# First attention of a two-layer cross-attention kernel: heads paired as neighbours, queries and keys of a pair by one product in a row half instead of two in quarters

## The reference, cut to what matters

```python
def _proj(W, b, x):
    return jnp.einsum('oi,bil->bol', W, x) + b[:, None]
q = _proj(Wq, bq, x_query)              # x_query = layernorm(x), (32, 64, 512)
k = _proj(Wk, bk, x_key)                # x_key = x_value = ctx
v = _proj(Wv, bv, x_value)
qh = q.reshape(B, D, h, Lh).transpose(2, 0, 1, 3)      # h = 8, Lh = 64, D = 64
scores = jnp.einsum('hbdk,hbek->hbde', qh, kh) * scale
p = jax.nn.softmax(scores, axis=-1)
xh = jnp.einsum('hbde,hbek->hbdk', p, vh)
x = xh.transpose(1, 2, 0, 3).reshape(B, D, L)
return _proj(Wo, bo, x)                 # added to x
```

## Time and profile before

| what | before |
|---|---|
| median of 3 runs | 810.43 us |
| the profiled execution | 810.15 us, its span 808.3 us, mean granted TensorE clock 0.941 |
| TensorE products busy | 687.0 us (85% of the span) |
| TensorE loads busy | 357.8 us (44%) |
| VectorE busy | 621.2 us (77%) |
| ScalarE busy | 483.1 us (60%) |
| GpSimd busy | 364.2 us (45%) |

### The profile page before, as it was taken

The page is one execution under the profiler, slowest core; times in us unless marked ns, Lnnn a source line. Parts: engine busy times, 40 slices in busy tenths (PEclk is TensorE's granted clock), DMA queues, the critical chain, the costliest instruction groups (busy, mean ns, idle before and its releaser), DMA issues. The chain is left out here.

```text
span 808.3 us, 17679 instructions
## 1 busy us (share of the span) xinstructions
PE 687.0 (85%) x6606; PEld 357.8 (44%) x6633; DVE 621.2 (77%) x1028; ACT 483.1 (60%) x873; POOL 364.2 (45%) x271
## 2 busy tenths in 40 slices
PE   2799999999977767499999479999999999479944
PEld 1345454554545555244444134444444444145541
DVE  4687788888636667499998579999999999355456
ACT  1687867667525657277777247787878787422100
POOL 1000008999925664022212146767777776343100
PEclk9999999999999999599999969999999999879955
DMA  5043555555442331023343100000000000035305
GB/s 149 27 136 111 200 186 147 157 147 154 89 126 77 72 82 30 15 56 74 74 71 70 37 0 1 2 2 0 2 1 2 2 1 1 1 72 85 53 2 208
DMA packets 94504, 54.98 MB, mean 68 GB/s; under 512 B 78868, under 2 KB 78868, under 8 KB 94420
## 3 DMA queue, kind: packets, MB, share of 16 engines
q1 hardware_dynamic: 93456, 53.71, 26.5%
q10 hardware_dynamic: 964, 0.13, 0.1%
HBM read 32.27 MB, written 4.19 MB: 45 GB/s over the span
## 5 line engine op out<-in xcount | busy, mean ns | idle before, releaser
L1314 POOL TENSOR_TENSOR query_qn<-query_eq,query_rq 128x1024 f32<-128x1024 f32 x64 | 121.7, 1902 | 56.6 <-DVE query_rq L1248 54.7
L610 ACT ACTIVATE keys_ek<-keys_psK,keys_mk 128x512 f32<-128x512 f32 x128 | 86.8, 684 | 39.8 <-DVE keys_mk L524 38.1
L524 DVE TENSOR_REDUCE keys_mk<-keys_psK 128x2 f32<-128x1024 f32 x64 | 77.9, 1217 | 22.5 <-PE keys_psK L662 21.7
L1239 DVE TENSOR_REDUCE query_mq<-query_psQ 128x16 bf16<-128x1024 f32 x64 | 75.6, 1181 | 5.0 <-PE query_psQ L1382 4.8
L1245 DVE TENSOR_REDUCE query_lq<-query_eq 128x16 f32<-128x1024 f32 x64 | 77.2, 1207 | 2.6 <-ACT query_eq L1323 2.5
L1323 ACT ACTIVATE query_eq<-query_psQ 128x1024 f32<-128x1024 f32 x64 | 65.2, 1018 | 22.6 <-PE query_psQ L1395 22.6
L1404 PE MATMUL query_psX<-all_ident,query_qn 128*128 128x128 f32 x512 | 70.4, 281 | 0.0
L673 PE MATMUL keys_psT<-all_ident,keys_ek 128*128 128x128 f32 x512 | 70.1, 280 | 0.0
L685 PE MATMUL keys_psG<-keys_eT,keys_cT 128*64 128x512 f32 x256 | 69.0, 617 | 1.0 <-issue 0.9
L1042 POOL TENSOR_SCALAR ff_hr<-ff_h,ff_qs 128x1376 f32<-128x1376 f32 x16 | 22.6, 1412 | 104.5 <-DVE ff_qs L1089 104.5
L673 PEld LDWEIGHTS keys_psT<-all_ident,keys_ek 128*128 128x128 f32 x512 | 54.8, 141 | 27.9 <-issue 21.3
(11 more groups left out here) (243 smaller groups left out, 1436.3 us busy)
## 6 DMA issues: line engine op xcount, KB each, us to landing
all_ring<-in_L_ffn_w_down_dram SPq DMA_DIRECT2D x8, 688.0 KB, 4.3
all_ring<-in_L_ffn_w_gate_dram SPq DMA_DIRECT2D x10, 512.0 KB, 6.6
all_ring<-in_L_ffn_w_up_dram SPq DMA_DIRECT2D x10, 512.0 KB, 3.7
all_cf<-in_ctx_dram SPq DMA_DIRECT2D x16, 256.0 KB, 2.7
all_x_res<-in_x_dram SPq DMA_DIRECT2D x4, 1024.0 KB, 6.2
att_ctx_n<-in_ctx_dram SPq DMA_DIRECT2D x16, 256.0 KB, 3.2
out_dram<-all_x_res SPq DMA_DIRECT2D x16, 256.0 KB, 2.2
att_w_nat<-in_L_ffn_W_dram SPq DMA_DIRECT2D x4, 256.0 KB, 4.2
```

What stands on the lines that cost most here:

```text
L524: dve.tensor_reduce(mk[:, c, :], psK[c % 2][:, :, :], X, ALU.max, negate=True).then_inc(mk_ok, 1)
L610: act.activation(ek[t % 2][b][:, c, :], psK[c % 2][:, b, :], ACT.Exp, bias=mk[:, c, b:b + 1], accum_out=le[t % 2][:, b, c:c + 1]).then_inc ...
L1239: dve.tensor_reduce(mq[g % 2][:, :, 0:HEADS], psQ[g % 2][:, :, :].rearrange("p b (h d) -> p b h d", d=D), X, ALU.max, negate=True).then_in ...
L1314: pool.tensor_tensor(qn[m % 2][:, :, :], eq[m % 3][:, :, :], rq[m % 2][:, :].unsqueeze(2).broadcast_to([P, 2 * HEADS, D]), ALU.mult).then_ ...
```

## The change

Heads are paired as neighbours: r is now the lower bit of the head, h = 2c + r, so that heads 2c and 2c+1 are 128 adjacent columns of xn and ctx_n. One product with these 128 columns as its stationary side gives both heads' queries (or keys), in 128 partitions of psQK. There are 16 such products per tile (8 for queries, 8 for keys) where there were 32, each in a row half of the array where each was in a quarter. `values` reads its 256 moving columns as four blocks of 64, 128 apart. `result` must put the heads back in their places: it is two instructions, one for each r, over 128 x 4 blocks of 64, and x_ok counts two per tile. Scores, W and O are as before; their operands are the same in shape.

```diff
@@ -818,7 +818,7 @@
             def stats(t):
-                dve.wait_ge(x_ok, t + 1)
+                dve.wait_ge(x_ok, 2 * t + 2)
...
@@ -842,10 +842,10 @@
             def result(t):
                 dve.wait_ge(o_ps, t + 1)
-                dve.scalar_tensor_tensor(out=k.x[:, t, :].rearrange("p (r n) -> p r n", r=2),
-                                         in0=psWO[:, :, NC * D:2 * NC * D], scalar=k.bo2[:, :],
-                                         in1=k.x[:, t, :].rearrange("p (r n) -> p r n", r=2),
-                                         op0=ALU.add, op1=ALU.add).then_inc(x_ok, 1)
+                heads = k.x[:, t, :].rearrange("p (c r n) -> p r c n", r=2, n=D)
+                for r in range(2):
+                    dve.scalar_tensor_tensor(out=heads[:, r], in0=psWO[:, r, NC * D:2 * NC * D].rearrange("p (c n) -> p c n", n=D),
+                                             scalar=k.bo2[:, :], in1=heads[:, r], op0=ALU.add, op1=ALU.add).then_inc(x_ok, 1)
...
@@ -916,10 +916,9 @@
                         for b in range(2):
-                            for r in range(2):
-                                at, h = (m * NC + c) * D, r * NC + c
-                                mm = pe.matmul(psQK[HALF[r], b, at:at + D], x[HALF[b], h * D:(h + 1) * D],
-                                               k.wT0[HALF[b], m, :], start=False, stop=True, skip_group_check=True)
+                            at = (m * NC + c) * D
+                            mm = pe.matmul(psQK[:, b, at:at + D], x[HALF[b], c * P:(c + 1) * P], k.wT0[HALF[b], m, :],
+                                           start=False, stop=True, skip_group_check=True)
...
@@ -927,7 +926,7 @@
                         mm = pe.matmul(psV[HALF[r], b, 0:NC * D], k.wT0[HALF[b], 2, :],
-                                       ctx_n[i % 2][HALF[b], r * NC * D:(r + 1) * NC * D],
+                                       ctx_n[i % 2][HALF[b], :].rearrange("p (c r n) -> p r c n", r=2, n=D)[:, r],
                                        start=True, stop=True)
...
@@ -943,7 +942,7 @@
                 pe.wait_ge(pn_ok, t + 1)
-                wait(pe, x_ok, t)
+                wait(pe, x_ok, 2 * t)
```

## The result

The changed kernel takes 813.27 us (median of 14 runs, 808.93 to 816.35), the kernel before beside it 810.21 us (14 runs, 808.89 to 811.86): 1.0036 times as long, 95% interval 1.002 to 1.0052. It is **slower by some 3 us**, where the prediction had it 2.3 us faster, and its times spread over 7.4 us where those of before spread over 3.0. The profiled execution took 811.93 us, its span 810.1.

What follows compares the result with a forecast made beforehand. The prediction took a TensorE chain of 5.36 us a tile, with code loading stalls of 16.1 us, to bound the attention stage. First tile +2.0, stage -4.5, results +0.2 gave -2.3 us: 808.1 us, range 797 to 816.

Steps and rivals of the forecast that it cites:

- rival 2: Code pieces on TensorE come late whatever is saved; half the loss per tile stays, +4.7 us, 815; chance 0.29.
- Q's own price: Q's loads and products in the first attention: 1.81 us instead of 0.98, 0.83 more per tile, +12.4 us in 15 tiles.
- rival 1: Q's longer loads hide, Q stays at 0.98 us, code loading bounds the tile at 4.35 us: 795; chance 0.17.
- rival 3: Q's halves load one after the other, 3.6 us for Q, +19.4 us in the stage: 835; chance 0.04.
- rival 4: Load and product of a half don't overlap, Q 2.8 us, +7.0 us in the stage: 821; chance 0.04.
- The first tile at the lower clock: First tile's Q loads, 1.66 us before, doubled in length to 3.62 us: +2.0 us.
- Idle time of "issue": TensorE's waits for code in the attention stage fall from 13.7 to some 3 us; 0.2 us per tile kept.
- Q to O: Another split of the array between Q and O on TensorE: 0, or 2.6 us if paid without ScalarE's copy as cover.
- the two results: VectorE's result in two instructions of 0.47 us: +0.20 us per tile, hidden except +0.2 us at the stage's end.
- the 0.17 us that I took from the bias after W: TensorE's idle time at the bias after W, 2.6 / 15 us per tile, as nearest row for a changed array split.
- The sum over the stage: Attention tiles S to S go from 5.36 to 5.06 us, over 15 tiles -4.5 us.
- rival 5: Products waiting for loads lower the clock for part of the attention stage; three such tiles, 817 us; chance 0.06.

Runs made afterwards that it cites:

- e1: Changed kernel with queries and keys back in quarters, rest of the change kept: 811.08 us, ratio 1.0016 against the kernel before.
- e4: Kernel before, in quarters, with SyncE's two weight transposes one tile later, each pair waiting for the pair before: 808.76 us, ratio 0.9983.
- l4_before: Third profile of the kernel before, no edit: 809.31 us.
- l1_after: Another profile of the changed kernel, no edit: 810.65 us.
- l2_after: Another profile of the changed kernel, no edit, the slowest of its four: 815.91 us.
- l3_before: Second profile of the kernel before, no edit: 810.97 us.
- e6: Changed kernel with weight transposes one tile later and tile 0's bias pair computed six times: 805.11 us, ratio 0.9944 against the kernel before.
- e2: Changed kernel with Q's loop over b outside that over c, half after half: 823.17 us, ratio 1.0162 against the kernel before.
- e3: Changed kernel with SyncE's two weight transposes one tile later, each pair waiting for the pair before: 809.17 us, ratio 1.0002 against the kernel before.
- e5: Changed kernel with the weight transposes one tile later, run again in another set: 807.67 us, ratio 0.9972 against the kernel before.
- e7: Changed kernel with tile 0's bias pair computed six times, transposes left in place: 807.58 us, ratio 0.9969 against the kernel before.

## Why the prediction was wrong

It said 808.1 us; the time is 813.27, slower instead of faster. That the range of 797 to 816 holds it is luck: its upper end was there for rival 2, whose mechanism did not come about. Each step:

- **Q's own price: right.** 1.93 us against 1.81, loads of 182 to 188 ns, starts of loads 0.11 us apart in a half and the halves side by side (16 loads per half in 1.93 us). Rivals 1, 3 and 4 (0.98, 3.6, 2.8 us) fall. The first tile at the lower clock cost +1.7 here and +1.8 between B0 and the first S on the means (7.56 in four profiles of the changed kernel against 5.72 in three of before), against +2.0.
- **Idle time of "issue": right, and short.** It went to nothing, not to 3 us; the 0.2 us per tile that I kept for it were not lost. Rival 2, the largest, falls. An undisturbed tile is 4.88 us where 4.03 + 0.83 gave 4.86, so 2.7 us in 15 tiles came out in its favour. What no run shows is the loading of code by itself; that 20 pieces became 16, and that the idle time comes back with the quarters (e1, e4), fits it; it is not shown.
- **Q to O, and the two results: right, at 0.** O starts at 252.19, before Q's last product ends (251.20 + 1.06), and W follows S by 253.98 - 253.38 = 0.60 us without a wait for x; the two results take 476 ns each, as forecast (0.47). But the 0.17 us that I took from the bias after W as the price of another split of the array was a misreading:

```profile
239.68 0.11 PEld L913 LDWEIGHTS att_psQK<-all_bias_rows,all_ones 128*128 128x128 bf16 x2
239.91 0.38 PE L913 MATMUL att_psQK<-all_bias_rows,all_ones 128*128 128x512 bf16 x1 [0.16 <-issue]
```

  That trace has two loads and one product of the pair, so the record of the first product is missing, and the idle time is its gap. l4_before has both products and no idle time there. The 1.0 us of e1 may lie in the two results (I gave it 0.2), or chance of the clock; not settled.
- **The sum over the stage: the step that failed**, "15 x (5.06 - 5.36) = -4.5". Over three profiles of before and four of the changed kernel the first S to the last went from 79.2 to 78.1 us on the mean: -1.1. By its parts: the 5.36 came from the slowest profile of three (1.3 us of gain that was not there); the 0.2 per tile was not needed (2.7 us in its favour); the late ctx_n was in no term and costs what four tiles are over 4.88, 3.9 us on the mean of the four profiles (4.1 in l1_after: 5.64, 5.11, 5.50, 7.34), of which 2.5 us are the waits themselves and most of the rest the spell of the lower clock behind one of them; another 1 us on the mean is tiles at the lower clock behind the first, 3.0 of it in l2_after (6.84 and 5.95 us). So -4.5 + 1.3 - 2.7 + 3.9 + 1.0 = -1.0.
- **What is late next was not asked of the transfers.** The row of the wait was there before (ctx_n, 2.2 us at the start; in l3_before, taken later, 1.8 us once inside the stage as well). I asked what bounds TensorE and not in which order SyncE issues.
- **The clock: rival 5, given 0.06, is part of the answer**, at other places than it named: not because the products wait for loads (e6 has Q in halves and 1.00 up to 316 us), but at the stage's start, where idle time brings the lower clock in both forms, and behind a late ctx_n. With it each Q costs some 3.5 us. The spell at the start lasts 3.4 to 6.8 us in five profiles with quarters; with halves 6.8 in four, and 17.1, 23.9 and 27.3 in three. The one profiled execution over 815 us has 17.1 us of it, which fits the long upper tail of the times; with the wait filled, one of eleven runs is still 3.7 us over its median.

The balance of the change, on the means of the profiles (2.2 us apart; the medians of the first sets are 3.1 apart, so 0.9 us are in no profile): B0 to first S +1.8, first S to last -1.1. The other +1.5 us lie in parts that the change does not touch: the stage began 0.9 us later, feed_forward to query_side took 129.4 us against 128.5, and the rest was 0.3 shorter. Forms with quarters show the longer feed_forward too (129.3 in e1, 129.4 in e4), when a spell of the lower clock falls on the last down products; so I do not count it as the change's, but whether the start of the stage can shift that spell stays open. Open as well: what the kernel before would gain from the filled start, which was not run; so how much of the 5.0 us of the best version is the halves' doing is not known. With the transposes later in both, halves and quarters are 1.1 us apart and not told from each other.

## What to carry to other kernels

When a change speeds up an engine that stalls now, walk the queue of each engine that feeds it, in its order of issue, and ask which transfer stands behind work of another stage: that is late next. Price a stall by several profiles, not one, when it varies by itself. And where TensorE waits a few us for a transfer and the clock falls, products that count for nothing, put into that wait, can be a cheap edit: here 2.2 us of them took the ratio from 1.0036 to 0.9969, some 5 us. Before a gap of 0.2 us is priced, compare the counts of loads and products beside it: a missing record looks like idle time.

## What the runs showed of the hardware

- Fp32 loads of 128 columns start 0.11 us apart in a half of the array, and two halves load side by side: in the program's order, b inside c, 32 of them with their products take 1.93 us.
- TensorE takes loads out of their order when they are for another part of the array (e2: those of ctx_n between those of xn, 0.05 us apart), and the products with them (one of ctx_n at 275.93, the next of xn at 276.04).
- The lower clock at the stage's start lasted 3.4 to 6.8 us with quarters (five profiles), 6.8 to 27.3 with halves (seven), and did not come in the two profiles where the idle wait for ctx_n ahead of Q was filled (against twelve of twelve without).
- In all four profiles of the changed kernel the longest wait for ctx_n inside the stage (0.9 to 1.6 us) was followed, within 2.4 us, by 3.4 us of the lower clock; where ctx_n was not late (e3, e5, e6) there was no such spell, and none behind the waits of 1.0 and 0.8 us of e7.
